# Attention and expert block on one core: the previous cell's output rows placed behind the third token product and the first running sum of the values

## The reference

```
z = cumlogsumexp(s, axis=time);  p = exp(s - z);  g = exp(z_previous - z)
hk_t = hk_(t-1) * g_t + k_t p_t ;  ok_t = q_t . hk_t          (64 x 64 per head)
pv  = softmax(ok, over the 64 slots)
hv_t = hv_(t-1) * g_t + p_t v_t ;  ov_t = pv_t . hv_t         (64 x 128 per head)
o = rmsnorm(ov) * g_norm_weight * (gate * sigmoid(gate))
x = layernorm(x + o.reshape(b, t, 2048) @ Wo)
```

## Time and profile before

| | |
|---|---|
| median of 3 runs | 1344.43 us (1342.18 to 1344.87) |
| the profiled execution: its time | 1344.9 us |
| its span, first to last instruction | 1343.2 us |
| PE busy | 1329.0 us, 99% |
| DVE, ACT, POOL busy | 820.8 us (61%), 472.3 us (35%), 276.5 us (21%) |
| chain that ended last | PE 96%, DVE 2%, DMA 1% |
| granted TensorE clock, mean | 0.997 of full speed |

### The profile page before, as it was taken

The page is one execution under the profiler, slowest core; times in us unless marked ns, Lnnn a source line. Parts: engine busy times, 40 slices in busy tenths (PEclk is TensorE's granted clock), DMA queues, the critical chain, the costliest instruction groups (busy, mean ns, idle before and its releaser), DMA issues.

```text
span 1343.2 us, 20338 instructions
## 1 busy us (share of the span) xinstructions
PE 1329.0 (99%) x8160; PEld 1140.7 (85%) x8160; DVE 820.8 (61%) x1559; ACT 472.3 (35%) x1391; POOL 276.5 (21%) x254
## 2 busy tenths in 40 slices
PE   8999999999999999999999999999999999999998
PEld 6888888888888888888888888888888888878886
DVE  5665666556666665566665566666555656756754
ACT  5333333343333433333324333333333333422221
POOL 3012311131112310231114111221122112212211
PEclk9999999999999999999999999999999999999999
DMA  6000200010000100010001000010000210000010
GB/s 204 17 1 0 56 1 16 1 35 22 16 1 24 32 17 1 18 39 17 1 0 48 9 16 1 25 32 17 1 24 24 64 32 1 2 0 32 16 47 32
DMA packets 35356, 31.73 MB, mean 24 GB/s; under 512 B 7616, under 2 KB 28096, under 8 KB 35264
## 3 DMA queue, kind: packets, MB, share of 16 engines
q1 hardware_dynamic: 35264, 30.44, 7.7%
HBM read 26.24 MB, written 4.19 MB: 23 GB/s over the span
## 4 chain that ended last, share of the span: by engine, by line
PE 96%; DVE 2%; DMA 1%; ACT 0%; issue 0%; POOL 0%; SPq 0%; POOLq 0%
PE p L879 19%; PE p L881 19%; PE p L880 19%; PE t L928 5%; PE s L953 3%; PE o L1069 3%; PE xb L1024 2%; PE o L1005 2%; PE o L1003 2%; PE p L953 2%; PE t L1069 2%; PE xb L978 2%; PE o L1002 2%; PE s L1371 2%; PE s L1372 2%; PE s L1373 2%
## 5 line engine op out<-in xcount | busy, mean ns | idle before, releaser
L879 PE MATMUL p<-wvg_hi,xt_hi 128*128 128x512 f32 x512 | 209.8, 410 | 0.0
L881 PE MATMUL p<-wvg_hi,xt_lo 128*128 128x512 f32 x512 | 200.9, 392 | 0.0
L880 PE MATMUL p<-wvg_lo,xt_hi 128*128 128x512 f32 x512 | 199.9, 390 | 0.0
L526 ACT ACTIVATE v_tok<-p 128x256 f32<-128x256 f32 x128 | 49.8, 389 | 328.8 <-PE p L881 328.8
L691 DVE SCALAR_TENSOR_TENSOR gate<-th,p 128x256 f32<-128x256 f32 x128 | 54.0, 422 | 164.2 <-ACT th L530 160.7
L879 PE MATMUL p<-xt_hi,wsqk_hi 128*128 128x512 f32 x380 | 148.4, 391 | 0.0
L880 PE MATMUL p<-xt_lo,wsqk_hi 128*128 128x512 f32 x380 | 148.2, 390 | 0.0
L881 PE MATMUL p<-xt_hi,wsqk_lo 128*128 128x512 f32 x380 | 147.8, 389 | 0.0
L475 POOL TENSOR_TENSOR orstd<-ovar,minus_half 128x8 f32<-128x8 f32 x32 | 52.5, 1640 | 447.4 <-DVE ovar L824 447.4
L466 POOL TENSOR_TENSOR v_lo<-v_tok,v_hi 128x256 fp32r<-128x256 f32 x96 | 83.6, 883 | 198.7 <-ACT v_hi L535 198.7
L881 PEld LDWEIGHTS p<-wvg_hi,xt_lo 128*128 128x128 f32 x512 | 96.1, 188 | 22.5
(11 more groups left out here) (241 smaller groups left out, 2846.5 us busy)
## 6 DMA issues: line engine op xcount, KB each, us to landing
raw<-in_L_attn_Wv SPq DMA_DIRECT2D x32, 128.0 KB, 2.4
raw<-in_L_attn_Wg SPq DMA_DIRECT2D x32, 128.0 KB, 3.0
raw<-in_L_attn_Wo SPq DMA_DIRECT2D x16, 256.0 KB, 2.8
out<-acc SPq DMA_DIRECT2D x16, 256.0 KB, 2.0
acc<-in_L_attn_hidden_states SPq DMA_DIRECT2D x3, 1024.0 KB, 8.0
raw<-in_L_attn_Ws SPq DMA_DIRECT2D x8, 256.0 KB, 2.8
raw<-in_L_attn_Wq SPq DMA_DIRECT2D x8, 256.0 KB, 2.9
raw<-in_L_attn_Wk SPq DMA_DIRECT2D x8, 256.0 KB, 3.0
```

What stands on the lines that cost most here:

```text
L526: nc.scalar.activation(v_tok[:, c, :], PB[bk][:, 0:VW], ACT.Copy).then_inc(v_done, 1)
L879: nc.tensor.matmul(out_, lh, rh, start=(k == 0), stop=False)
L880: nc.tensor.matmul(out_, lh, rl, start=False, stop=False)
L881: last = nc.tensor.matmul(out_, ll, rh, start=False, stop=(k == n - 1))
```

## The change

It does four things. (1) On PE token product 2 and running sum 0 of the values come directly behind the products of the slots, and the four output rows of the preceding cell behind them; `P_USES` has `vg2` ahead of `wo0`. The uses' waits move with it: `wo1` now waits for the gate of chunk 2, `wo2` for the sum of `wo0`, `wo3` for that of `wo1`, `vg3` for that of `wo2`. (2) On DVE the gate of chunk 2 and the first copy of `hv` come directly behind the subtraction of the maximum, ahead of pz; all four sums of output rows come behind pz, two ahead of `esum` and two behind `esq`. (3) On ACT, in the last cell alone, the splitting of the first two tables comes behind chunk 2's values. (4) Bank names for the last cell and the stage behind it follow the new order. No instruction is added or taken away.

```
-P_USES = ["vg0", "vg1", "wo0", "wo1", "wo2", "wo3", "vg2", "vg3", "s", "q", "k", "a0", "a1"]
+P_USES = ["vg0", "vg1", "vg2", "wo0", "wo1", "wo2", "wo3", "vg3", "s", "q", "k", "a0", "a1"]
...
-        bank_v0, bank_v1 = [PB[p_turn(Cell(None, CELLS - 1), use)[0]] for use in ("vg2", "vg3")]
+        bank_v0, bank_v1 = [PB[p_turn(Cell(None, CELLS - 1), use)[0]] for use in ("wo3", "vg3")]
...
             nc.scalar.activation(flat, flat, ACT.Exp).then_inc(exp_done, 1)
-            if last:
-                car.prep_high(act, 0, PREP[0])
-                car.prep_high(act, 1, PREP[1])
             if cell.b == CELLS - 2:
                 for kt in range(KT):
                     car.w1_high(act, kt)
             values_scalar(act, cell, 2)
             values_high(act, cell, 2)
+            if last:
+                car.prep_high(act, 0, PREP[0])
+                car.prep_high(act, 1, PREP[1])
...
             nc.vector.tensor_reduce(top[:], groups, AX_X, ALU.max).then_inc(top_done, 1)
-            if not first(cell):
-                add_rows(dve, cell, 0)
...
-            if not first(cell):
-                add_rows(dve, cell, 1)
-            else:
-                keep_values(0)
+            gate_vector(dve, cell, 2)
+            keep_values(0)
...
             if not first(cell):
-                add_rows(dve, cell, 2)
+                add_rows(dve, cell, 0)
+                add_rows(dve, cell, 1)
             nc.vector.tensor_reduce(esum[:], groups, AX_X, ALU.add).then_inc(esum_done, 1)
...
             if not first(cell):
+                add_rows(dve, cell, 2)
                 add_rows(dve, cell, 3)
             for c in range(CH - 1):
-                if c > 0 or not first(cell):
+                if c > 0:
                     keep_values(c)
...
-                if c < 2:
-                    gate_vector(dve, cell, c + 2)
+                if c == 1:
+                    gate_vector(dve, cell, 3)
...
             mm.then_inc(ok_summed, 1)
-            if not first(cell):
-                for c in range(CH):
-                    output_rows(pe, cell, c)
-            if last:
-                car.prep_turn(pe, 0, PREP[0])
-                car.prep_turn(pe, 1, PREP[1])
...
+            token_proj(pe, cell, 2)
             running_values(0)
-            token_proj(pe, cell, 2)
+            if not first(cell):
+                for c in range(CH):
+                    output_rows(pe, cell, c)
+            if last:
+                car.prep_turn(pe, 0, PREP[0])
+                car.prep_turn(pe, 1, PREP[1])
             running_values(1)
...
-                        pe.wait_ge(gate_done, cell.count(CH, CH - 1))
+                        pe.wait_ge(added, cell.count(CH, 0))
```

## The result

| | before | after |
|---|---|---|
| median | 1344.59 us (4 runs) | 1361.89 us (1361.39 to 1362.35, 4 runs) |
| ratio | | 1.0131, 95% interval 1.0115 to 1.0147 |
| span of the profiled execution | 1343.2 us | 1360.3 us |
| PE busy | 1329.0 us | 1339.2 us |

A forecast was written before the change was run, and what follows sets the result against it. PE, busy all through a middle cell, was taken to bound the kernel. Losses of 9.9 (29 cells x 0.34), 1.5, 3.8 and 0.5 sum to 15.7 us, taking the profiled 1344.9 to 1360.6; forecast median 1360, range 1353 to 1367.

The forecast's parts named there:

- What bounds the kernel: Whole attention: PE is busy throughout and waits only in single cells, so a new order can win a few tenths at most.
- Running sum 0: All cells but 0: v_lo of chunk 0 waits for DVE's subtraction and comes late, costing 0.34 us a cell.
- The signs named: Expected in the profile: PE waits for v_lo in about 30 cells, a 36.4 us cell, waits in cells 0 and 30.
- The Trainium skill's rule: VectorE with two SBUF inputs and GpSimd reading SBUF exclude each other, the second fully blocking; a cell would lose 0.48 us.
- rival 2: More lost a cell: full exclusion (0.48 us), or pz meets the third v_lo, the sum 0.15 later; 1364 us, chance 0.2.
- The bank of `wo2`: wo2 waits for the sum of wo0, done at 434.51 against a load at 434.57: just fits, no added loss.
- Cells 0 and 30: Single losses: cell 0 1.5 us, running sum 1 waiting for hv; cell 30 3.8 us, W1's splitting and batch 0's statistics.
- Cell 31: Usual 0.34 us plus 0.3 for table transposes awaiting a low half, partly offset by the old 0.2 end wait: 0.5 us.
- The rest of the sum: 29 cells at 0.34 us make 9.9; with 1.5, 3.8 and 0.5 the loss is 15.7 us, nothing elsewhere.

The follow-up runs named there:

- run 4: Changed kernel with e_tok_lo early, v_lo of chunk 1 late and the sums of wo0 and wo1 ahead of pz: 1349.42 us, ratio 1.0042.
- Runs 1: Changed kernel with the high half of e_tok and POOL's e_tok_lo ahead of the second high half of y: 1369.34 us.
- 2: Changed kernel with e_tok_lo early and the high half of v for chunk 1 behind chunk 2's tanh on ACT, cell 0 excepted: 1360.29 us.
- 7: Changed kernel with e_tok_lo computed twice on POOL: 1389.49 us.
- 3: Changed kernel with the sums of wo0 and wo1 ahead of pz on DVE: 1361.28 us.
- run 5: Changed kernel with PE's and DVE's old order in cell 0, and W1's splitting and batch 0's statistics later in cell 30: 1355.51 us.
- Run 11: The changed kernel itself, executed again for a second profile: 1363.14 us.
- run 9: Changed kernel with the edits of run 4 and run 5 together: 1345.79 us, ratio 1.0014.
- run 10: As run 9, and in cell 31 two tables turned ahead of the output rows, their low halves ahead of the fourth sum: 1345.44 us, ratio 1.0013.

## Why the prediction was right, point by point

**What bounds the kernel**: right. PE had next to no waits to lose (the lists of before have one more in the attention that the text passes over, 0.3 us for xt_lo at the start of cell 0), and run 4 shows that the same instructions in the new order take the same 36.05 us once nothing is late.

**Running sum 0** (0.34 forecast): 0.358 in the first profile. The steps came out one by one: the subtraction drawn 0.72 us long, 0.03 of it waiting (forecast 0.04), v_lo of chunk 0 ending 3.04 us behind the slots' products (forecast 3.05), the load 0.06 behind it (0.05), an unhidden load's surcharge of 0.1 (0.08). Runs 1, 2 and 7 show the mechanism by moving it.

**The signs named.** The subtraction of 0.7 us, 0.55 sooner against the maximum, the first v_lo of 1.2 and the cell of 36.4 all came. The wait at running sum 0 came in 31 cells, but in the list of the weight loads and not in PE's. In cell 30 `wo1` waited 1.15 us for its gate: that is over the 0.5 that was to prove the forecast wrong, but the text had foreseen it for this cell, and in the middle cells `wo1`, `wo3` and `vg3` had no wait.

**The Trainium skill's rule** of full exclusion ("SBUF — State Buffer", the summary's rules for kernel authors): the rows agree again but for the last 0.14 to 0.15 us. In the change v_lo, at its own 0.74, must have got going at 435.20, and the subtraction ended at 435.34. The prediction's 0.48 a cell counts that overlap as lost only where v_lo follows the subtraction; the subtraction follows e_tok_lo by the same rule, so the rule's own words give 0.62 a cell, and with that rival 2 stands at about 1368 instead of 1364. Neither came. Nor did the other half of rival 2: pz meets the third v_lo only in its last 0.13 us and takes 0.69.

**The bank of `wo2`**, "it just fits": right, with 0.04 us between the load as due (439.00) and as made (439.04). But the text made less of it than it is worth. That two chains end together means that neither mend alone helps, which runs 2 and 3 then showed.

**Cells 0 and 30** (1.5 and 3.8): 1.55 and 3.86. In cell 30 the two causes were forecast as 2.3 and 1.5; run 5 undid them together, so their shares are read from the waits and were not tried apart.

**Cell 31** (0.5): 0.97. This term was sized too small, by its two parts. The tables' transposes lost about 0.6 us, not 0.3: by the rows' distances the third starts 0.35 late, behind a low half, and the product after the fourth another 0.2. And the old wait at the cell's end was to give 0.2 back; it did go, but 0.20 us for the copies `hv` came in its place. These are no later than before: the product that needs them starts 1.67 us behind the fourth v_tok in both kernels. Before, the wait for the low half had hidden most of theirs, and only its weight load shows a rest of it. In the kernel before:

```profile
1163.89 0.38 ACT L526 ACTIVATE v_tok<-p 128x256 f32<-128x256 f32 x1 [1.99 <-PE p L881]
...
1165.56 0.18 PEld L1053 LDWEIGHTS o<-hv,pz_t 64*128 64x128 f32 x1 [0.18 <-DVE hv L746]
```

And after:

```profile
1175.87 1.25 PE L138 MATMUL s<-ident,v_raw 128*128 128x128 f32 x8 [0.18 <-DVE vt_lo L147]
...
1179.93 0.38 ACT L526 ACTIVATE v_tok<-p 128x256 f32<-128x256 f32 x1 [2.17 <-PE p L879]
...
1181.60 0.37 PE L1051 MATMUL o<-hv,pz_t 64*128 64x128 f32 x1 [0.20 <-DVE hv L746]
```

**The rest of the sum**: the stage behind the attention was taken as unchanged and was 1.06 us longer in the first profile. Run 11 has 172.86 there, as before the change had: the change has no part in it (below). The terms that are the change's own came to 16.8 us in the first profile and 17.3 in run 11, against the 15.7 of the sum: 0.5 us of the difference is cell 31, the rest mostly the middle cells, which lost 0.02 to 0.04 us more each than was forecast.

## What to carry to other kernels

Where the busiest engine has no waits, as here, a new order of its work had nothing to win and could only lose; ask of every moved instruction when its operand and its bank are ready, on the other engines' new order and not on their old one. When two chains end within a few hundredths of a microsecond of each other, undo both before you call either harmless. And look for waits shorter than a matmul's drawn length in the waits of the weight loads, and measure them by the distance from one round of the loop to the next: the idle time between matmuls doesn't show them.

## What the runs showed of the hardware that was not expected

**POOL and DVE by turns.** That instructions of the two exclude each other was forecast; that the wait is per instruction and so strong was seen in run 9, where pz, starting with the second of POOL's four instructions (1.27 us), took 1.82 us for 0.69 of work, and POOL's third instruction then took 1.72. Instructions of DVE with one input in PSUM ran beside POOL at their usual length (`acc` 0.69, `hv` 0.58).

**The clock behind a wait.** In the expert stage PE waits once for 3.3 us (for `w_pad`), in every kernel here. In the 12 us from 22 us into that stage the granted clock was 0.72 in the change's first profile, 0.86 in its second, 0.86 before, and 1.00 in run 10; the stage took 173.9, 172.9, 172.8 and 171.2 us. The wait ends 25.2 us into the stage in all four, and the second round of the product behind it starts 66.8, 65.8, 65.8 and 64.2 us into it, so the whole difference lies between. The first and the last, windows view (in the same busy time PE starts 29 matmuls in the one and 43 in the other):

```profile
1208.42:1220.42 12.00, 8.78 (x29) 7.00 (x30) 2.73 (x10) 0.60 (x1) 1.01 (x2) 0.72 0.00 0
```
```profile
1193.08:1205.08 12.00, 8.76 (x43) 7.03 (x44) 5.01 (x16) 1.02 (x3) 1.03 (x2) 1.00 0.00 0
```

After the same wait PE is given, in part of that stretch, the lower of its two clock levels (1.2 of 2.4 GHz) for more or less time, or not at all. That is up to 2.7 us between executions whose instructions there are the same, as much as the difference that a measurement of this kernel can tell from none, and it covers the 1.06 us that the change's first profile had beyond the account.
